# Attention with a mixture of experts on one core: the output projection of each head group on two 64-row halves of the array, in two steps; its four token tiles in four PSUM banks; a transposed tile moved to the projection's bank; the router's products one score pair later

## The reference, cut to what matters

```python
def attn(x, W_qkv, W_out, s):                    # x: 4 x 512 x 256, 8 kv heads, 4 query heads each, HD = 64
    q, k, v = split(x @ W_qkv);  q, k = rope(q), rope(k)
    a = einsum('bqhmd,bkhd->bhmqk', q, k) / 8
    a = where((q_pos >= k_pos) & (q_pos < k_pos + 64), -inf, a)
    w = softmax(concat([a, s]))[..., :-1]         # s: a learned sink logit for each head
    return einsum('bhmqk,bkhd->bqhmd', w, v).reshape(B, L, 2048) @ W_out
x = x + attn(layernorm(x))
x = x + moe(layernorm(x))    # 8 experts, top 2, 640 slots each, hidden 1024; slots given in order of tokens
```

## Time and profile before

| | |
|---|---|
| median of 3 runs | 1142.63 us (1141.35 to 1145.35) |
| the profiled execution's own time | 1137.98 us |
| its span | 1136.2 us |
| busy in the span | PE 94%, DVE 77%, ACT 57%, POOL 63% |
| attention | until about 851 us |
| a full period | 24.92 to 24.99 us, without routing beside it |

### The profile page before, as it was taken

How to read it: one execution, slowest core, us unless ns; L and a number is a source line. 1 busy time by engine, 2 the same in 40 slices (tenths; PEclk the granted TensorE clock), 3 DMA queues, 4 the chain that set the end, 5 groups by cost and what they waited for, 6 DMA issues and landing times.

```text
span 1136.2 us, 30831 instructions
## 1 busy us (share of the span) xinstructions
PE 1064.9 (94%) x12411; PEld 725.5 (64%) x12411; DVE 876.8 (77%) x1915; ACT 647.3 (57%) x1530; POOL 714.0 (63%) x612
## 2 busy tenths in 40 slices
PE   5799999999999999999999999999982899999995
PEld 3355555555655555565555555655552899999995
DVE  7999888889898888988988898898853554444442
ACT  3556666667656666775665567566533544444541
POOL 4676665666668776666887666678614255666662
PEclk9899999999999999999999999999996899999998
DMA  3454444433233332322333333232413244444331
GB/s 102 132 148 113 123 128 112 127 90 94 76 89 103 103 102 79 93 74 75 93 104 107 79 93 96 76 88 77 145 36 114 104 118 118 104 101 100 97 86 20
DMA packets 115391, 111.33 MB, mean 98 GB/s; under 512 B 35216, under 2 KB 103888, under 8 KB 115120
## 3 DMA queue, kind: packets, MB, share of 16 engines
q1 hardware_dynamic: 107952, 100.81, 30.4%
q0 software_dynamic: 7296, 8.55, 4.5%
HBM read 74.17 MB, written 21.83 MB: 84 GB/s over the span
## 4 chain that ended last, share of the span: by engine, by line
PE 81%; DVE 14%; issue 3%; DMA 1%; POOL 1%; ACT 0%; POOLq 0%; DVEq 0%
PE bank L1251 21%; PE bank L1272 21%; PE bank L1382 10%; PE bank L1225 10%; PE bank L1395 9%; PE bank L1287 7%; DVE probs_ring L951 4%; DVE probs_t L960 4%; DVE heads_sb L982 2%; PE bank L1360 1%; PE bank L1232 1%; PE bank L1325 0%; POOL slot_rows L703 0%; DVE swap_sb L1010 0%; DMA slots<-slot_rows 0%
## 5 line engine op out<-in xcount | busy, mean ns | idle before, releaser
L776 ACT ACTIVATE probs_ring<-probs_ring,neg_max 128x512 f32<-128x512 f32 x512 | 366.7, 717 | 262.4 <-DVE neg_max L951 261.2
L951 DVE CUSTOM_DVE_ANT_0 probs_ring<-bank,mask,sink_neg 128x512 f32<-128x512 f32 x512 | 364.5, 737 | 81.4 <-PE bank L1251 79.7
L960 DVE STREAM_TRANSPOSE probs_t<-probs_ring 128x1024 f32<-128x1024 f32 x256 | 317.2, 1239 | 0.0
L1251 PE MATMUL bank<-qk_st 64*128 64x512 f32 x1024 | 291.1, 645 | 19.0 <-DVE neg_max L951 16.4
L1272 PE MATMUL bank<-probs_t,v_quads 32*64 32x256 f32 x8192 | 247.9, 381 | 3.0 <-DVE probs_t L960 2.4
L1272 PEld LDWEIGHTS bank<-probs_t,v_quads 32*64 32x64 f32 x8192 | 179.6, 132 | 79.5 <-issue 49.9
L645 POOL TENSOR_TENSOR x_sb<-x_sb,y_sb 128x512 f32<-128x512 f32 x62 | 79.5, 1282 | 202.7 <-ACT y_sb L786 202.6
L1251 PEld LDWEIGHTS bank<-qk_st 64*128 64x128 f32 x1024 | 77.7, 186 | 111.9 <-issue 72.8
L623 POOL TENSOR_TENSOR chunk_sb<-chunk_sb,rope_sb 128x512 f32<-128x512 f32 (+1 forms) x94 | 120.7, 1284 | 28.0 <-DMA swap_sb<-chunk_sb 27.4
L1225 PE MATMUL bank<-xcur,w_hi 128*128 128x512 f32 x384 | 132.4, 426 | 3.4 <-POOL w_lo L589 1.8
L1287 PEld LDWEIGHTS bank<-wo_sb,heads_sb 128*128 128x128 f32 x512 | 92.1, 189 | 58.4 <-issue 46.2
(11 more groups left out here) (147 smaller groups left out, 1463.1 us busy)
## 6 DMA issues: line engine op xcount, KB each, us to landing
v_quads<-v_rows SPq DMA_DIRECT2D x128, 128.0 KB
recip_wide<-recip_rows SPq DMA_DIRECT2D x64, 256.0 KB, 4.4
w_raw<-in_L_ffn_w SPq DMA_DIRECT2D x16, 1024.0 KB, 6.2
swap_sb<-chunk_sb SPq DMA_DIRECT2D x314, 32.0 KB, 2.0
w_raw<-in_L_attn_W_qkv SPq DMA_DIRECT2D x32, 256.0 KB, 2.9
slot_rows<-x2T SPq DMA_DIRECT2D x8, 662.5 KB, 5.4
slots<-slot_rows SPq DMA_DIRECT2D x8, 662.5 KB, 4.0
w_raw<-in_L_attn_W_qkv SPq DMA_DIRECT2D x64, 64.0 KB, 2.7
```

The lines of the kernel that those rows point to most:

```text
L776: nc.scalar.activation(probs[n % RING][:, :], probs[n % RING][:, :], ACT.Exp, bias=neg_max[j][:, n:n + 1], scale=-1.0, accum_out=sums[j][: ...
L951: nc.vector.tensor_tensor_reduce(probs[n % RING][:, :], SCORE[SCORE_OF[n // 2][n % 2]][:, :], mask[:, L - P - t * P:2 * L - P - t * P], -S ...
L960: nc.vector.transpose(probs_t[j][:, :, (h // 2) * (2 * P):(h // 2 + 1) * (2 * P)] .rearrange("p b (h q) -> p h b q", h=2)[:, :, :, t * BLK ...
L1251: nc.tensor.matmul(SCORE[SCORE_OF[n // 2][hh]][:, :], qk_st[j][half, h // 2, t * P:(t + 1) * P], qk_st[j][half, PAIRS, :], start=True, sto ...
```

## The change

- Y (all groups but the last) is made by 64-row matmuls, 16 for each group in place of 8: `heads_sb[rows, a]` by `wo_sb[rows]`, with the upper and the lower two heads on the two halves of the array. Step one gives each token tile one half of the sum, step two the other. Each tile a has a bank of its own, `PV[a]`, so the two halves of the array write different banks; step two waits (`s_y_part`) for step one.
- DVE multiplies all four tiles of `heads_sb` at step 26. ACT takes Y out in four copies of 128 x 256 at step 31, where it took two of 128 x 512 at steps 29 and 31. POOL adds both parts at step 31, tiles 0 and 2, then 1 and 3. Waits on `s_heads` that kept `PV` banks free become waits on `s_y_out`.
- The late tile is turned in `PROJ`. So it waits for `chunk_out` of Q23, and projection KV at step 0 of the next period waits for DVE's `norm_lo`; PV no longer does.
- Routing: turning x moves from step 0 to 2, its copies from steps 1 and 2 to 3 and 4, logits and counts from step 0 to 2, and what follows by one to two steps.
- For the last batch the statistics of tiles 0 and 1 stand between the two residual adds.
- Transfers are the same, in the same order.

```diff
@@ -308,5 +309,6 @@
         SINK_AT, DENOM_AT, RECIP_AT = 16, 17, 18
-        HEADS_AT = {26: 0, 27: 1}
+        HEADS_AT = 26
         Y_AT = {28: 0, 30: 1}
-        RESIDUAL_AT = {29: 0, 31: 1}
+        Y_OUT_AT = 31
+        LAST_RESIDUAL_AT = {29: 0, 31: 1}
 
@@ -335,11 +337,11 @@
         VAR_AT, STD_AT, RSTD_AT = 16 + 8, 16 + 9, 16 + 11
-        TURN_X_AT = 32
-        X2T_AT = {33: 0, 34: 1}
-        NORM2_AT = {35: 0, 36: 1, 38: 2, 40: 3}
+        TURN_X_AT = 34
+        X2T_AT = {35: 0, 36: 1}
+        NORM2_AT = {37: 0, 38: 1, 40: 2, 42: 3}
         IDS_AT, MEAN_PART_AT = 41, 42
-        LOGITS_AT, CENTRE_AT, SCALE_AT = 48, 49, 50
-        TOP_AT, SHIFT_AT, INDEX_AT, GATE_EXP_AT, ONEHOT_AT, CHOSEN_AT = 51, 52, 52, 53, 54, 55
-        GATE_SUM_AT, GATES_AT, TOP_SUM_AT, WEIGHTS_AT = 56, 58, 62, 70
-        COUNT_AT = 64
-        PLACE_AT, PICK_AT, SLOT_AT, INDICES_AT = 65, 66, 68, 69
+        LOGITS_AT, CENTRE_AT, SCALE_AT = 50, 51, 52
+        TOP_AT, SHIFT_AT, INDEX_AT, GATE_EXP_AT, ONEHOT_AT, CHOSEN_AT = 53, 54, 54, 55, 56, 57
+        GATE_SUM_AT, GATES_AT, TOP_SUM_AT, WEIGHTS_AT = 58, 60, 63, 71
+        COUNT_AT = 66
+        PLACE_AT, PICK_AT, SLOT_AT, INDICES_AT = 67, 68, 70, 71
         SCATTER_AT = {75: 0, 76: 1, 78: 2, 91: 3, 92: 4, 94: 5, 107: 6, 108: 7}
@@ -395,3 +397,3 @@
 
-            return NORM_BANKS[n] if n < TPB else PV[3]
+            return NORM_BANKS[n] if n < TPB else PROJ
 
@@ -638,10 +640,10 @@
 
-                if n in RESIDUAL_AT and g < GROUPS - 1:
-                    half = RESIDUAL_AT[n]
-                    pool.wait_ge(s_y_out, 2 * g + half + 1)
-                    if later(2 * g + half):
-                        pool.wait_ge(s_residual, 2 * g + half)
-                    t = (g // NKV) * TPB + 2 * half
-                    nc.gpsimd.tensor_tensor(x_sb[:, t:t + 2, :], x_sb[:, t:t + 2, :], y_sb[half][:, :, :],
-                                            ALU.add).then_inc(s_residual, 1)
+                if n == Y_OUT_AT and g < GROUPS - 1:
+                    for odd in range(2):
+                        pool.wait_ge(s_y_out, 2 * g + odd + 1)
+                        if later(2 * g + odd):
+                            pool.wait_ge(s_residual, 2 * g + odd)
+                        t = (g // NKV) * TPB + odd
+                        nc.gpsimd.tensor_tensor(x_sb[:, t:t + 3:2, :], x_sb[:, t:t + 3:2, :], y_sb[odd][:, :, :],
+                                                ALU.add).then_inc(s_residual, 1)
 
@@ -778,11 +780,12 @@
                                          accum_out=sums[j][:, n:n + 1]).then_inc(s_probs, 1)
-                if n in RESIDUAL_AT and g < GROUPS - 1:
-                    half = RESIDUAL_AT[n]
-                    act.wait_ge(s_y, 2 * g + half + 1 + 1)
-                    if later(g):
-                        act.wait_ge(s_residual, 2 * g + half - 1)
-                    if half == 0 and g + 1 in LATE_PERIODS:
-                        act.wait_ge(s_norm_turned, TPB + LATE_PERIODS.index(g + 1) + 1)
-                    nc.scalar.activation(y_sb[half][:, :, :], PV[half][:, :].rearrange("p (t d) -> p t d", t=2),
-                                         ACT.Copy).then_inc(s_y_out, 1)
+                if n == Y_OUT_AT and g < GROUPS - 1:
+                    act.wait_ge(s_y, 2 * g + 2 + 1)
+                    for odd in range(2):
+                        if later(g):
+                            act.wait_ge(s_residual, 2 * g + odd - 1)
+                        if odd == 0 and g + 1 in LATE_PERIODS:
+                            act.wait_ge(s_norm_turned, TPB + LATE_PERIODS.index(g + 1) + 1)
+                        for second in range(2):
+                            ins = nc.scalar.activation(y_sb[odd][:, second, :], PV[2 * second + odd][:, 0:D], ACT.Copy)
+                        ins.then_inc(s_y_out, 1)
                 if n == SINK_AT:
@@ -973,10 +976,8 @@
                     nc.vector.transpose(recip_t[:, :], recip[:, :]).then_inc(s_recip, 1)
-                if n in HEADS_AT:
-                    half = HEADS_AT[n]
-                    if half == 0:
-                        dve.wait_ge(s_pv, g + 1 + 1)
-                        dve.wait_ge(s_recip_in, g * 32 + 32)
-                        if later(2 * g):
-                            dve.wait_ge(s_y, 2 * g + 1)
-                    for a in (2 * half, 2 * half + 1):
+                if n == HEADS_AT:
+                    dve.wait_ge(s_pv, g + 1 + 1)
+                    dve.wait_ge(s_recip_in, g * 32 + 32)
+                    if later(2 * g):
+                        dve.wait_ge(s_y, 2 * g + 1)
+                    for a in range(QUADS):
                         ins = nc.vector.tensor_tensor(
@@ -985,5 +986,6 @@
                             recip_wide[:, a, :].rearrange("p (h t i) -> p h t i", h=2, i=BLK), ALU.mult)
-                    ins.then_inc(s_heads, 1)
-                if n in RESIDUAL_AT and g == GROUPS - 1:
-                    half = RESIDUAL_AT[n]
+                        if a % 2 == 1:
+                            ins.then_inc(s_heads, 1)
+                if n in LAST_RESIDUAL_AT and g == GROUPS - 1:
+                    half = LAST_RESIDUAL_AT[n]
                     t = (B - 1) * TPB + 2 * half
@@ -994,2 +996,8 @@
                                             ALU.add).then_inc(s_residual, 1)
+                    if half == 0:
+                        dve.wait_ge(s_norm2, (B - 1) * TPB)
+                    dve.wait_ge(s_residual, 2 * g + half + 1)
+                    for a in (2 * half, 2 * half + 1):
+                        ln(nc.vector.bn_stats(stats[:, a, :], x_sb[:, (B - 1) * TPB + a, :]))
+                        ln(nc.vector.bn_aggr(mean_var[:, a, :], stats[:, a, :]))
             nc.vector.memset(recip[:, :], 0.0)
@@ -1032,3 +1040,3 @@
 
-                if r in STATS_AT:
+                if r in STATS_AT and not last:
                     t = STATS_AT[r]
@@ -1036,3 +1044,3 @@
                         dve.wait_ge(s_norm2, b * TPB)
-                    dve.wait_ge(s_residual, b * (2 * NKV) + (2 * NKV - 1 + t // 2))
+                    dve.wait_ge(s_residual, b * (2 * NKV) + (2 * NKV - 1 + t % 2))
                     ln(nc.vector.bn_stats(stats[:, t, :], x_sb[:, b * TPB + t, :]))
@@ -1209,3 +1217,3 @@
                 if m in LATE_TURN_AT:
-                    pe.wait_ge(s_heads, 2 * (m // UNITS) + 1)
+                    pe.wait_ge(s_chunk_out, (m // UNITS + 1) * CHUNKS + Q23 + 1)
                     turn_norm(TPB + LATE_TURN_AT[m])
@@ -1217,3 +1225,6 @@
 
-                    pe.wait_ge(s_xT_lo, (g // NKV + 1) * TPB)
+                    if g - 2 in LATE_PERIODS:
+                        pe.wait_ge(s_xT_lo, TPB + LATE_PERIODS.index(g - 2) + 1)
+                    else:
+                        pe.wait_ge(s_xT_lo, (g // NKV + 1) * TPB)
                 if c == Q23:
@@ -1258,4 +1269,2 @@
                             pe.wait_ge(s_y_out, 2 * g)
-                        if g in LATE_PERIODS:
-                            pe.wait_ge(s_xT_lo, TPB + LATE_PERIODS.index(g) + 1)
                         if g % NKV == 1 and g > NKV:
@@ -1281,12 +1290,25 @@
                     half = Y_AT[n]
-                    pe.wait_ge(s_heads, 2 * g + half + 1 + 1)
+                    pe.wait_ge(s_heads, 2 * g + (half if g == GROUPS - 1 else 1) + 1 + 1)
                     if g < NKV and half == 0:
                         pe.wait_ge(s_wo_in, (g + 1) * (16 * PAIRS))
-                    for a in (2 * half, 2 * half + 1):
-                        for h in range(2):
-                            ins = nc.tensor.matmul(
-                                PV[half][:, (a % 2) * D:(a % 2 + 1) * D], heads_sb[:, a, h * P:(h + 1) * P],
-                                wo_sb[:, bass.ds((g % NKV) * 2 + h, 1), :].rearrange("p a n -> p (a n)"),
-                                start=(h == 0), stop=(h == 1))
-                    ins.then_inc(s_y, 1)
+                    if g == GROUPS - 1:
+                        for a in (2 * half, 2 * half + 1):
+                            for h in range(2):
+                                ins = nc.tensor.matmul(
+                                    PV[half][:, (a % 2) * D:(a % 2 + 1) * D], heads_sb[:, a, h * P:(h + 1) * P],
+                                    wo_sb[:, (g % NKV) * 2 + h, :], start=(h == 0), stop=(h == 1))
+                        ins.then_inc(s_y, 1)
+                    else:
+                        if half == 1:
+                            pe.wait_ge(s_y_part, 2 * g + 2)
+                        for second in range(2):
+                            for h in range(2):
+                                for p in range(PAIRS):
+                                    a, rows = 2 * second + (p + half) % 2, slice(p * HD, (p + 1) * HD)
+                                    ins = nc.tensor.matmul(
+                                        PV[a][:, 0:D], heads_sb[rows, a, h * P:(h + 1) * P],
+                                        wo_sb[rows, (g % NKV) * 2 + h, :],
```

(10 more changed lines are left out.)

11 lines of the change are left out of this document (9 added, 2 removed).

## The result

The changed kernel takes 1187.24 us (median of 4 runs, 1184.29 to 1191.57) against 1143.08 us (4 runs, 1141.35 to 1145.35) before: a ratio of 1.039, 95% interval 1.035 to 1.043. The forecast had the sign, slower, but 16.8 us of it; 44 us came. The time lies above the upper end of the range, 1168.

A forecast was written before the change was run, and what follows sets the result against it. PE's queue was taken as the bound, DVE just behind. 1137.98 - 2.5 (plain) + 5.8 (late) + 11.5 (routing) + 3 (clock) - 1.0 (end) = 1154.8 us, +16.8; on the median's scale 1159.4 us, range 1147 to 1168.

The forecast's parts named there:

- Shape of the array, Y, plain period: Y on half rows takes 1.73 us, not 1.93; pair 14 still waits for DVE; a plain period gains 0.28 us.
- 4 x 0.19: Four changes of array shape vanish in a plain period; PE alone would save 0.78 us.
- Late period: Projection KV waits for DVE's norm_lo: 0.48 us lost in each of 12 periods, 5.8 us.
- Period 10: Routing periods 10, 18, 26: PV waits for ACT's x2T copies, 3.8 us each, 11.5 us in three batches.
- half clock: Granted clock of 0.50 after the routing stall: 0 to 1.7 us each, taken as 1.0, 3 us in all.
- The failed step: Logits and counts one pair later on PE cost nothing, but for perhaps 0.4 us once in period 28, left out.
- End: Last batch: statistics of two of four tiles lie beside the second Y half, about -1.0 us.
- rival 1: Shape changes pay everywhere, as DVE and ACT always keep ahead: -19.5 us, 1123 us; chance 0.08.
- 3: Rival: the two Y halves do not overlap, 1.73 us more in each of 62 Y steps: 1250 us; chance 0.03.
- rival 2: No stall in routing, and gains of 0.7 us in nine periods meet the wait for norm_lo: 1141 us; chance 0.06.
- signs of being right: Y of 1.73 us with 379 ns matmuls; late KV idle until DVE; PV idle some 4 us behind x2T, then half clock.
- none of being wrong: PV within 1 us of the score pair ahead, Y above 2 us, or pair 14 before DVE's unit 12.

The follow-up runs named there:

- r6: The changed kernel with routing's steps as before, both late-tile splits one step earlier, and Y on all 128 rows again: 1145.9 us, 1.0041 of the kernel before.
- r4: The changed kernel with ACT's rounding and DVE's split of the late tile one step earlier: 1177.84 us (one run).
- r10: The changed kernel with only POOL's scaling, shift and pick issued at their old steps, ahead of the rotations: 1168.03 us (one run).
- r8: The changed kernel with routing's steps as before, late splits one step earlier, POOL's second residual add behind the denominator: 1136.6 us, 0.9964 of the kernel before.
- r1: The changed kernel with every step of routing where it was before the change: 1146.46 us (9 runs), 1.0056 of the kernel before.

## Why the prediction was wrong in size

- **Shape of the array, Y, plain period: right.** Y 1.73 us as forecast, no gain at pair 14, -0.38 us where -0.28 stood. r6 shows that it is the half rows. (The forecast's 4 x 0.19 makes 0.76 and not 0.78; nothing hangs on it.)
- **Late period: right.** +0.50 us against +0.48, behind DVE's split as named; r4 shows it by removal. Five of the twelve lose less, so the sum is 4.8 where 5.8 stood; period 7 had taken 25.49 us already before, above the 24.99 given as the upper end of a full period.
- **Period 10: right in mechanism, a term mis-sized.** PV came 4.5 us later where 3.8 stood, mostly because POOL's two adds put off `chunk_out` by 1.55 us and not 1.0. The half clock raises the period to +5.6 to +7.0 where 4.8 stood, 4 us too little over three. Its price was taken as 1.0 us and bounded at 1.7: PV alone took 3.86 us in place of 2.41 under 3.4 us of half clock, and in period 18 it lasted 6.8 us and cost 1.4 us more.
- **The failed step** is the sentence "Logits and counts stand on PE as before, one pair later; their results come to DVE after its transpose at step 3, which in period 28 may cost PE 0.4 us once, left out". It followed PE and DVE and left out the third queue of the same chain: the scaling and the pick are POOL's, and moving them from step 2 to step 4 carries them past the rotation of KV at step 3 and the weight split issued with it (the shift, `gates`, goes past that of Q01). That is 6.45 us of queue for 0.24 us of work. Where the forecast had -0.28 us for each logits period and nothing for the counts, these six periods cost 21.1 us; r10 gives back 17.6 of them by the order of POOL alone. Of the 29.6 us that the forecast lacks (46.4 against 16.8 in the profiled executions) 22 are this step, 4 are period 10 and 4 the end.
- **End: wrong sign.** "Two of four now lie beside the second Y half: about -1.0 us" came true for the place of the statistics but gained nothing, as ACT's `std` is not earlier (r8). And the slots are turned on PE 2.5 us later (48.39 us after the last score pair against 45.93). The forecast had seen that the adds delay `sink_arg` and `denom` and wrote that DVE "makes that good during PV"; in the last group no PV of a next one covers it. The last heads products start 1.3 us later (16.51 us against 15.20), and under the half clock they take 5.24 us and not 3.55. r8, without that delay, has neither.
- **Rivals.** Neither rival 1 nor 3 came; rival 2's absent stall would have needed routing's old steps, and with them (r1) the result is +0.6%, not -0.1%, since the late periods and the end still cost, and a plain period gained 0.38 us and not 0.7.
- **The signs.** All that the forecast named as signs of being right came (the matmuls of Y at 376 ns where 379 stood), and none of being wrong. They covered only the steps that it had looked at.

Period 18 lost 1.4 us more than 10, and 19 lost 1.6 less than 11. The granted clock accounts for it: it was 0.50 for 6.8 us in period 18 (508.0 to 514.9) and for 3.4 us in 10 and 26, and for 3.4 us in 11 and 27 but not at all in 19, whose 3.3 us are the bare stall. In r4, with the same stalls, the parts are changed over: periods 10 and 26 have 6.8 us of it and take 32.7 and 32.9 us, 11 and 27 have none and take 29.9; 18 and 19 have 3.4 us each and take 31.7 and 31.5. So this is not a property of period 18. What decides how long the clock stays down is open.

## What to carry to other kernels

When a step moves, list every engine that has a job in its chain, and in each of those queues what the job is moved past; a 0.24 us job behind 6 us of unhurried work costs 5 us on the engine that waits at its queue's head. Then do the same for the place where nothing follows, the last pass, as slack that hides a delay elsewhere is missing there. Judge the parts of a change apart: here half rows gained 4.5 to 6 us, and the moved steps that came with them cost about 40.

## What was not expected of the hardware

- A short stall costs twice: behind 4.30 us idle, 16 matmuls ran 5.41 us and not 3.72, and the granted clock was 0.50 (1.2 of 2.4 GHz) for 3.4 us or more behind the stalls of periods 10, 18 and 26, and in period 11 behind 3.30 us idle (327.11 to 330.52).
- Two profiled executions can differ where their kernels don't. Periods 0 and 1 took 24.37 + 25.06 us in the changed kernel and 26.98 + 27.73 in r1, 5.3 us more, though r1 differs only in routing, from period 10 on. The clock is what differs: in r1 the first matmuls of the projection after pair 0 still take 1.22 us, where they take 0.73 in the changed kernel, and from 50.4 to 57.2 us the granted clock was 0.50 in r1 and 1.00 in the changed kernel. Spans of single executions therefore don't rank kernels that are 3 us apart; the periods inside them do.
